# Turning layer 1's probabilities on the vector engine in 32x32 blocks instead of on the tensor engine

## The reference

```
qh = (layer_norm(x) @ wq + bq).reshape(b, q_len, 16, 128)
kh = (ctx @ wk + bk).reshape(b, t, 16, 128);  vh likewise with wv, bv
kh, vh = concatenate([kh, bias_k]), concatenate([vh, bias_v])      # 64 + 1 keys
weights = softmax(einsum('bqhk,bthk->bhqt', qh, kh) / sqrt(128))
x = x + einsum('bhqt,bthk->bqhk', weights, vh).reshape(b, q_len, 2048) @ wo + bo
```

## Time and profile before

| | before |
|---|---|
| time, median of 3 runs | 1775.13 us (1770.52 to 1775.52) |
| profiled execution, its own time | 1776.97 us |
| span of the profiled execution | 1775.3 us |
| mean granted TensorE clock | 0.948 of full |
| PE busy | 1599.1 us (90%) |
| PEld busy | 1360.9 us (77%) |
| DVE busy | 922.6 us (52%) |
| ACT busy | 726.8 us (41%) |
| POOL busy | 405.7 us (23%) |

### The profile page before, as it was taken

One profiled execution on the slowest core, in us unless ns is written; L12 is line 12 of the kernel. 1 busy time (PEld: TensorE's weight loads), 2 busy tenths in 40 slices (PEclk: granted clock), 3 DMA queues, 4 the chain that ended last, 5 costly groups with the idle time before them and its releaser, 6 DMA issues. The chain is left out here.

```text
span 1775.3 us, 33085 instructions
## 1 busy us (share of the span) xinstructions
PE 1599.1 (90%) x13486; PEld 1360.9 (77%) x13486; DVE 922.6 (52%) x1926; ACT 726.8 (41%) x1335; POOL 405.7 (23%) x430
## 2 busy tenths in 40 slices
PE   5978999999999969999999999689789849999498
PEld 3656888888888848888888888669667638887397
DVE  6874444343535454343434444674499964454743
ACT  4653434343444334434353434332256523332421
POOL 2012020010210030110200200260188853321600
PEclk9988999999999989999999999889899969999699
DMA  3021010010000030000100100100300000000001
GB/s 100 1 62 46 1 48 1 7 43 1 25 13 1 1 107 1 25 25 1 48 2 1 37 1 1 51 19 0 75 1 1 1 32 27 2 3 2 1 1 47
DMA packets 48462, 38.23 MB, mean 22 GB/s; under 512 B 10626, under 2 KB 45384, under 8 KB 48200
## 3 DMA queue, kind: packets, MB, share of 16 engines
q1 hardware_dynamic: 48328, 36.30, 6.9%
HBM read 34.20 MB, written 2.10 MB: 20 GB/s over the span
## 5 line engine op out<-in xcount | busy, mean ns | idle before, releaser
L939 DVE TENSOR_REDUCE att_rmax<-psum 128x6 f32<-128x390 f32 (+1 forms) x96 | 49.2, 512 | 401.4 <-PE psum L771 401.4
L914 ACT ACTIVATE att_q_sb<-psum,split_cols 128x512 f32<-128x512 f32 x128 | 88.1, 688 | 295.8 <-PE psum L807 295.1
L852 PE MATMUL psum<-att_wo_hi,att_ot_hi 128*128 128x256 f32 x512 | 149.4, 292 | 2.8 <-DVE att_ot_lo L968 2.8
L852 PE MATMUL psum<-att_wo_lo,att_ot_hi 128*128 128x256 f32 x512 | 144.8, 283 | 0.0
L852 PE MATMUL psum<-att_wo_hi,att_ot_lo 128*128 128x256 f32 x512 | 144.8, 283 | 0.0
L835 PE MATMUL psum<-att_pt,att_v_sb 128*128 128x128 f32 x1024 | 122.2, 278 | 1.0 <-ACT att_pt L923 1.0
L835 PEld LDWEIGHTS psum<-att_pt,att_v_sb 128*128 128x128 f32 x1024 | 116.8, 192 | 3.2 <-issue 1.5
L917 ACT ACTIVATE att_k_sb<-psum,split_cols 128x512 f32<-128x512 f32 x128 | 88.2, 689 | 71.4 <-PE psum L807 71.4
L807 PE MATMUL psum<-split_feat_hi,att_wqk_hi 128*128 128x512 f32 x256 | 105.5, 412 | 12.8 <-DVE att_pt L933 12.8
L977 DVE TENSOR_TENSOR g_x_res<-psum,g_x_res 128x256 f32<-128x256 f32 x128 | 54.3, 424 | 110.6 <-PE psum L852 77.7
L721 POOL CAST att_wqk_hi<-w_stage_qk 128x512 fp32r<-128x512 f32 x28 | 17.2, 613 | 401.7 <-PE psum L807 398.9
(11 more groups left out here) (294 smaller groups left out, 4042.5 us busy)
## 6 DMA issues: line engine op xcount, KB each, us to landing
ln_wo<-in_L_xattn_wo SPq DMA_DIRECT2D x2, 2048.0 KB
w_stage_qk<-in_L_xattn_wq SPq DMA_DIRECT2D x32, 128.0 KB, 2.2
w_stage_qk<-in_L_xattn_wk SPq DMA_DIRECT2D x32, 128.0 KB, 2.5
w_stage_vo<-in_L_xattn_wv SPq DMA_DIRECT2D x8, 512.0 KB, 3.8
w_stage_vo<-in_L_xattn_wo SPq DMA_DIRECT2D x8, 512.0 KB, 4.0
c_ctx_tok<-in_ctx SPq DMA_DIRECT2D x4, 512.0 KB, 5.3
g_x_res<-in_x SPq DMA_DIRECT2D x4, 512.0 KB, 8.6
m_w<-in_L_xattn_w_fc SPq DMA_DIRECT2D x2, 1024.0 KB, 6.1
```

The costliest lines, as they stand in the source:

```text
L852: mm = pe.matmul(o_ps[p % 2], a, b, start=(h == 0 and t == 0), stop=(not last and h == HG - 1 and t == 2))
L914: act.activation(q_sb[:, h, :], q_ps[:, :], ACT.Identity, bias=G.cols[:, i - 1, head:head + 1]).then_inc(q_ready, 1)
L939: dve.tensor_reduce(rmax[:, a:b], s_ps[group][:, :, :], X_AXIS, ALU.max).then_inc(max_done, 1)
```

## The change

PE's `turn` and ACT's four copies go. DVE gets a `turn` of its own at the end of each iteration that has a new step: 16 block transposes, SBUF to SBUF, one for each of the four quadrants of 32 source partitions times two sequences of a pair times two halves of the keys. Each takes 32 partitions x 8 chunks x 32 columns (256 float32 columns) and writes the 32x32 blocks turned into their place in `pt`. The semaphore `t_psum` goes; `pt_ready` is raised once a step; the waits on `ot_ready` and `x_added` move from PE's `turn` to the head of PE's `context`, which now waits for the whole of `pt` before its first head. The block below is the core of it.

```diff
-                def turn(j, pair):
-                    pe.wait_ge(prob_ready, len(GROUPS) * j + pair + 2)
-                    if j:
-                        pe.wait_ge(ot_ready, HG * j)
-                        pe.wait_ge(x_added, PPB * j)
-                    for h in range(2):
-                        for pp in range(2):
-                            n = PPB * (2 * pair + h) + 2 * pp
-                            mm = pe.transpose(t_ps[pair][:, h, pp, :], prob[:, n:n + 2, :].rearrange("p c t -> p (c t)"), G.ident[:, :])
-                    mm.then_inc(t_psum, 1)
...
                     pe.wait_ge(k_ready, HG * min(j + 2, NI))
+                    pe.wait_ge(pt_ready, j + 1)
+                    if j:
+                        pe.wait_ge(ot_ready, HG * j)
+                        pe.wait_ge(x_added, PPB * j)
                     for h in range(HG):
-                        pe.wait_ge(pt_ready, 4 * j + 2 * (h // 2) + 2 if h < 2 else 4 * j + 4)
...
-                        if h == 2 and 1 <= j <= NI:
-                            turn(j - 1, 0)
-                            turn(j - 1, 1)
...
-                        for pair in range(2 if h == 2 and 1 <= j <= NI else 0):
-                            act.wait_ge(t_psum, 2 * (j - 1) + pair + 1)
-                            for u in range(2):
-                                half = slice(T * u, T * u + T)
-                                act.activation(pt[half, 2 * pair:2 * pair + 2, :, :, u, :].rearrange("p h a r t -> p (h a r) t"),
-                                               t_ps[pair][half, :, :, :].rearrange("p h a (r t) -> p (h a r) t", r=2),
-                                               ACT.Copy).then_inc(pt_ready, 1)
...
-                    if j:
-                        dve.wait_ge(t_psum, 2 * j)
                     dve.tensor_tensor(prob[:, a:b, :], soft[:, a:b, 0:T],
...
+                def turn(j):
+                    dve.wait_ge(prob_ready, len(GROUPS) * (j + 1))
+                    if j:
+                        dve.wait_ge(c_psum, HG * j)
+                    by_pair = prob[:, :, :].rearrange("p (n u) t -> p n u t", u=2)
+                    for r in range(2):
+                        for u in range(2):
+                            for a in range(2):
+                                for c in range(2):
+                                    of, to = T * r + 32 * a, T * u + 32 * c
+                                    turned = dve.transpose(pt[to:to + 32, :, :, r, u, 32 * a:32 * a + 32].rearrange("p h a t -> p (h a) t"),
+                                                           by_pair[of:of + 32, :, u, 32 * c:32 * c + 32])
+                    turned.then_inc(pt_ready, 1)
...
                     if old:
                         for p in range(PPB):
                             add_output(j - 2, p)
+                    if new:
+                        turn(j - 1)
```

More of the change, by code:

```diff
@@ L685, in phase_layer1_attention @@
             ("vo_in", "wqk_ready", "wv_ready", "wo_ready", "kb_ready"))
-        q_psum, k_psum, v_psum, s_psum, t_psum, c_psum, o_psum, bt_psum = (m.sem(n) for n in
-            ("q_psum", "k_psum", "v_psum", "s_psum", "t_psum", "c_psum", "o_psum", "bt_psum"))
+        q_psum, k_psum, v_psum, s_psum, c_psum, o_psum, bt_psum = (m.sem(n) for n in
+            ("q_psum", "k_psum", "v_psum", "s_psum", "c_psum", "o_psum", "bt_psum"))
         q_ready, k_ready, pt_ready, ot_high, ot_ready, x_added, bt_done = (m.sem(n) for n in
```

## The result

| | before | after |
|---|---|---|
| median (5 runs each) | 1774.07 us | 1762.04 us |
| lowest to highest | 1770.52 to 1775.52 | 1760.36 to 1766.36 |
| profiled execution, its own time | 1776.97 us | 1760.36 us |

The ratio is 0.9941 with a 95% interval of 0.9928 to 0.9955: 12 us, or 0.6%, faster. The forecast was 1761 us (1752 to 1773).

A forecast was written before the change was run, and what follows sets the result against it. PE's instruction stream was taken as the bound inside the attention calls. Loop gain and end costs, -26.5 + 2 x (4.0 + 2.2) = -14.1 us from 1776.97, gave 1762.8, a median of 1761 us (1752 to 1773).

The forecast's parts named there:

- The bound: Inside the attention calls PE's instruction stream is the bound; removing its 8 transposes saves 0.885 us an iteration, 26.5 us.
- ACT's copies at nothing: Removing ACT's four copies, 2.4 us a step, gains nothing inside the loop, since PE does not wait for ACT there.
- The price of a transpose, d: Start-to-start time of one DVE block transpose, taken as 0.35 us, so 5.6 us for the 16 of a turn.
- Hidden in the loop: DVE's turn fits its idle hole before the first scores, 11.6 us after the change, and costs 0 inside the loop.
- The circle that I worked out for its failure: Turn, first maximum to second value copy, fourth value product to last output addition: 15.2 + 16 d, binding from 16 d = 13.0 us.
- The ends, waiting: At each call's end nothing hides DVE's turn, so `context` starts 16 d - 1.6 later, +4.0 us with d = 0.35.
- The ends, clock: At each call's end PE idles over 5 us, its clock falls, and half-speed work costs 2.2 us an end.
- The sum: Whole kernel: -26.5 + 2 x (4.0 + 2.2) = -14.1 us, giving 1762.8 us for the profiled execution, 1761 us for the median.
- B: Rival: a DVE transpose takes about 0.60 us, hidden in the loop but 10.3 us an end; 1769 us, chance 0.16.
- A: The forecast itself: 1761 us; 1757 if the clock holds, 1765 with 3.0 us an end and d = 0.42; chance 0.70.
- C: Rival: DVE's transposes become the bound, the loop gains only some 3 us, slower than before at 1801 us; chance 0.10.
- D: Rival: PE's gap between head 2 and head 3 does not close, only the ends count, +12 us, 1787; chance 0.04.

The follow-up runs named there:

- the run with 32 transposes: The kernel after with each DVE turn inside the loop done twice (same result, one wait between), at the ends once: 1839.16 us (1836.23 to 1839.44).

## Why the prediction was right

- **The bound.** Right. PE's stream was the bound inside the calls, and an iteration shrank by 0.87 us (0.885 forecast). 30 x 0.87 = 26.1 us; the run with the transposes put back measured 26.6.
- **ACT's copies at nothing.** Right, shown by the same run.
- **The price of a transpose, d.** Too low: 0.35 us forecast, 0.449 measured, inside the bounds of 0.19 and 0.86. The multiplication's rate and the 0.01 us allowed for turning were right: the record is 0.435 us where the multiplication's is 0.425. Wrong was the overlap of 0.09 us subtracted from it, because each transpose writes to other partitions than the one before. The figure of 311 ns in "VectorE: DVE Perf Modes", section "The three transpose paths" of the Trainium skill, taken per column, gave 0.62 us and was too high. Read as a fixed part plus the multiplication's rate it gives, as an estimate, 0.178 + 0.266 = 0.44 us for the record, and the trace agrees with 0.435.
- **Hidden in the loop.** Right, with idle of 4.54 us left where "about 6" was forecast. The circle that I worked out for its failure was incomplete (it binds too, but only in the last steps of a call): it went through the bank that a value copy frees and left out the one through `pt_ready`, the wait that the change itself adds. Its limit is a turn of 28.24 - 15.8 = 12.4 us, not 13.0. Of the 32 us by which the run with 32 transposes missed its forecast, 15 to 16 come of it (30.22 us an iteration instead of 29.7); of the rest, some 11 are the clock.
- **The ends, waiting.** The formula 16 d - 1.6 holds: with 7.2 us of transposes it gives 5.6, measured 7.91 - 2.17 = 5.7 us. With my d it gave 4.0.
- **The ends, clock.** Right in kind, 2.2 us forecast, 1.4 and 1.5 us measured, and up to 2.7 in the kernel whose ends alone are turned by DVE. It fell during the idle as forecast, and filling the idle kept it up.
- **The sum.** The two errors at the ends lean opposite ways, 1.7 us too little waiting and 0.75 us too much clock an end. By the measured terms it is -26.1 + 2 x (5.7 + 1.45) = -11.8 us, against 12.0 between the medians and 11.1 in the two calls of the traces. The forecast's -14.1 met the time within 1 us partly because it set out from 1775.13, while the median of before is now 1774.07.
- **The rivals.** B is out as a price (0.60 us), though d came out at 0.449, where its range began (0.45) and beyond the 0.42 allowed to A; that the time still met A's is luck in part: the smaller loss of clock and the higher starting value made up for it. C is out by the 4.54 us of idle, D by the closed gap.

## What to carry to other kernels

When an engine's stream is the bound, moving an instruction off it pays the distance between starts, not its busy time, and the other engine's busy time is free up to a circle of waits that can be added up beforehand; each wait that the change adds starts a circle of its own, so add up that one first. A price for a row of short instructions is taken from rows that follow each other in the same way: here the record of an instruction was right to 0.01 us, and whether the next one overlaps it decided the rest. The bill for moved work comes where the pipeline drains: there the longer path stands bare, and an idle bound engine also loses its clock. It can pay to have two forms of the same step, the one that relieves the bound engine inside the loop and the one with the short latency at its end: here that turned 12 us into 29.

## What was not expected of the hardware

- A DVE transpose was not disturbed by POOL: all 512 lie between 415 and 442 ns, and so do the 114 that ran while POOL was at work. The elementwise maximum of two SBUF operands in the same place was: a turn of 6.86 us became 9.64 to 10.98 us beside POOL, and single instructions took up to 2.5 us. Whether the second operand or the operation makes the difference these runs do not tell. In this respect the transpose was the safer choice for the hole, which it shares with POOL's work.
- Where a DVE instruction on 32 partitions wrote to other partitions than the one before it, its start came 0.08 us later (0.42 us for 256 float32 columns instead of 0.34). Moving the data to partitions other than those it was read from cost nothing that shows, and neither did breaking the 256 columns in 8 pieces.
